# Two-layer graph kernel: ScalarE takes the statistics of the first edge layer's rows, and VectorE's scales go to the end of its turn

## What is computed

```python
def reference(x, src, dst, edge_type_8, L0_gnn_weight, L0_gnn_bias, L1_gnn_W_self, L1_gnn_W_neigh):
    def _L0_gnn_ref(x, edge_index, edge_type, weight, bias):
        row, col = (edge_index[0], edge_index[1])
        xt = jnp.einsum('ni,rio->rno', x, weight)
        messages = xt[edge_type, col]
        out = jax.ops.segment_sum(messages, row, num_segments=num_nodes)
        return jax.nn.relu(out + bias)
    ...
    h = jnp.maximum(_layernorm(x, axis=-1), 0.0)
    x = x + _L0_gnn_ref(h, edge_index, edge_type_8, L0_gnn_weight, L0_gnn_bias)
    h = jnp.maximum(_layernorm(x, axis=-1), 0.0)
    x = x + _L1_gnn_ref(h, L1_gnn_W_self, L1_gnn_W_neigh, src, dst)
    return x
```

## Time and profile before

| | before |
|---|---|
| median of 3 runs | 3427.87 us (3419.07 to 3433.84) |
| profiled execution, its own time | 3424.89 us |
| its span | 3423.2 us |
| granted TensorE clock, mean | 0.912 |
| PE busy | 2528.3 us (74%) |
| DVE busy | 3036.0 us (89%) |
| ACT busy | 2198.9 us (64%) |
| POOL busy | 2461.4 us (72%) |

### The profile page before, as it was taken

The page is one execution under the profiler, slowest core; times in us unless marked ns, Lnnn a source line. Parts: engine busy times, 40 slices in busy tenths (PEclk is TensorE's granted clock), DMA queues, the critical chain, the costliest instruction groups (busy, mean ns, idle before and its releaser), DMA issues.

```text
span 3423.2 us, 64727 instructions
## 1 busy us (share of the span) xinstructions
PE 2528.3 (74%) x10740; PEld 1658.5 (48%) x10741; DVE 3036.0 (89%) x13368; ACT 2198.9 (64%) x6002; POOL 2461.4 (72%) x1732
## 2 busy tenths in 40 slices
PE   3665766767788888888777777777777775777787
PEld 1224655555566666666533333333333333565565
DVE  8999778888899999999789999999999997777777
ACT  5994233323333333333379999999999995777776
POOL 0004886767788888888678888888888885777775
PEclk8998888888899999999989999999999998999989
DMA  9702466666655555555544545445455453889897
GB/s 364 285 0 52 80 116 150 144 139 152 127 105 106 103 106 103 106 103 106 84 155 175 194 173 189 178 173 194 172 186 181 174 190 145 295 285 303 285 306 252
DMA packets 308089, 576.91 MB, mean 169 GB/s; under 512 B 32095, under 2 KB 188034, under 8 KB 307982
## 3 DMA queue, kind: packets, MB, share of 16 engines
q1 hardware_dynamic: 212366, 419.40, 35.9%
q0 software_dynamic: 95616, 156.31, 23.5%
HBM read 316.70 MB, written 258.88 MB: 168 GB/s over the span
## 4 chain that ended last, share of the span: by engine, by line
DVE 45%; issue 24%; PE 15%; DMA 7%; POOL 5%; DVEq 2%; ACT 1%; POOLq 1%; ACTq 0%; SPq 0%
DVE best L1165 6%; DVE w L1172 6%; DVE zone_c L1172 6%; PE banks L1574 5%; DMA agg<-msg,sidx 4%; PE banks L1474 4%; DMA w<-hs,gidx 2%; POOL w L734 2%; PE banks L1416 2%; DVE zone_c L846 2%; DVE zone_c L1050 2%; DVE zone_c L1054 2%; DVE zone_c L848 2%; DVE zone_c L1200 2%; DVE zone_c L1052 2%
## 5 line engine op out<-in xcount | busy, mean ns | idle before, releaser
L1546 PE MATMUL banks<-w,hT 128*128 128x512 f32 x1568 | 764.5, 645 | 252.2 <-ACT hT L1326 247.7
L667 POOL DMA_INDIRECT agg<-msg,sidx x400 | 667.1, 1668 | 185.2 <-issue 123.0
L655 POOL DMA_INDIRECT rows_in<-in_x,gidx x400 | 433.4, 1084 | 414.9 <-DVE gidx L871 280.5
L1546 PEld LDWEIGHTS banks<-w,hT 128*128 128x128 f32 x1568 | 312.8, 204 | 646.0 <-issue 508.7
L1200 DVE SCALAR_TENSOR_TENSOR zone_c<-banks,rdeg,zone_c 128x256 f32 x784 | 379.3, 484 | 158.6 <-PE banks L1574 123.1
L1574 PE MATMUL banks<-w,zone_c 128*128 x1568 | 405.5, 417 | 143.2 <-POOLq L742 113.8
L1416 PE MATMUL banks<-pick,h 128*128 128x128 f32 x1600 | 286.3, 307 | 301.1 <-ACT h L1217 206.1
L1474 PE MATMUL banks<-w,hT 128*128 x1600 | 482.7, 430 | 16.5 <-issue 15.1
L1235 ACT COPY msg<-banks 128x256 f32<-128x256 f32 x400 | 148.2, 370 | 510.9 <-PE banks L1485 486.5
L734 POOL DMA_INDIRECT w<-hs,gidx x392 | 372.5, 950 | 143.5 <-issue 93.8
L1416 PEld LDWEIGHTS banks<-pick,h 128*128 128x128 f32 x1600 | 256.1, 214 | 365.2 <-issue 343.1
(11 more groups left out here) (229 smaller groups left out, 5793.9 us busy)
## 6 DMA issues: line engine op xcount, KB each, us to landing
out_rows<-zone_c SPq DMA_DIRECT2D x196, 512.0 KB, 2.7
agg<-bias SPq DMA_DIRECT2D x2, 25344.0 KB, 97.4
zone_c<-agg SPq DMA_DIRECT2D x98, 512.0 KB, 6.1
hs<-zone_c SPq DMA_DIRECT2D x98, 512.0 KB, 3.6
zone_c<-out_rows SPq DMA_DIRECT2D x98, 512.0 KB, 5.9
rows_in<-in_x SPq DMA_DIRECT2D x97, 512.0 KB, 5.4
keyrow<-key_rows SPq DMA_DIRECT2D x100, 320.0 KB, 3.9
zone_c<-bucket_rows SPq DMA_DIRECT2D x28, 448.0 KB
```

The lines of the kernel that those rows point to most:

```text
L655: pool.indirect_dma_start(out=rows_in[p][:, j, :], out_offset=None, in_=x[:, :], in_offset=bass.IndirectOffsetOnAxis(ap=gidx[p][:, j:j + 1 ...
L667: pool.indirect_dma_start(out=agg[:, :], out_offset=bass.IndirectOffsetOnAxis(ap=sidx[p][:, j:j + 1], axis=0), in_=msg[p][:, j * D:(j + 1) ...
L1546: last = mm(bank[4 + j][:, :], hT[p][:, c, j * P:(j + 1) * P], w1[:, c, :], start=(c == 0), stop=(c == KC - 1))
```

## The change

ScalarE computes the statistics of the first edge layer with three passes over the gathered rows: `edge0_mean` (a copy with a sum, and the sum scaled to minus the mean), `edge0_deviation` (squares with a sum, and std), `edge0_normal` (h, as before). The mean stands behind the third eviction, deviation and normalised tiles behind the fourth. VectorE's bn_stats and bn_aggr go. Its copy of the gather indices, the reciprocal and the shift form `edge0_scales`, which stands at the end of its turn, behind the side work. The mean pass writes its copy into `h`, the square pass into `act_junk`.

```diff
--- before.py
+++ after.py
@@ -269,8 +269,6 @@
         extra = two("extra", [P, B])
         met = two("met", [P, B])
         livekey = two("livekey", [P, B])
-        stats = two("stats", [P, B, 6])
-        mv = two("mv", [P, B, 2])
         std = two("std", [P, B])
         rstd = two("rstd", [P, B])
         shift = two("shift", [P, B])
@@ -392,7 +390,8 @@
         staged0 = sem("staged0")
         node_hot = sem("node_hot")
         degrees0 = sem("degrees0")
-        stats0 = sem("stats0")
+        sum0 = sem("sum0")
+        mean0 = sem("mean0")
         var0 = sem("var0")
         std0 = sem("std0")
         recip0 = sem("recip0")
@@ -894,22 +893,6 @@
             dve.wait_ge(pe_done, 6)
             v.tensor_copy(btype[:, :], bank[3][0:1, 0:SLOTS]).then_inc(btype_done, 1)
 
-            def statistics(b, p, source, stats_sem, var_sem):
-                for j in range(B):
-                    last = v.bn_stats(stats[p][:, j, :], source[p][:, j, :])
-                last.then_inc(stats_sem, 1)
-                wait_alone(dve, stats_sem, b + 1)
-                for j in range(B):
-                    last = v.bn_aggr(mv[p][:, j, :], stats[p][:, j, :])
-                last.then_inc(var_sem, 1)
-
-            def scales(b, p, std_sem, recip_sem, done):
-                dve.wait_ge(std_sem, b + 1)
-                v.reciprocal(rstd[p][:, :], std[p][:, :]).then_inc(recip_sem, 1)
-                dve.wait_ge(recip_sem, b + 1)
-                v.scalar_tensor_tensor(shift[p][:, :], mv[p][:, :, 0], -1.0, rstd[p][:, :], ALU.mult,
-                                       ALU.mult).then_inc(done, 1)
-
 
             def edge0_front(b, r, p):
                 wait_from(dve, sidx0, b - 1, b, 2)
@@ -936,11 +919,15 @@
                                        ALU.mult).then_inc(live0, 1)
                 dve.wait_ge(live0, 2 * b + 1)
                 v.tensor_tensor(livekey[p][:, :], extra[p][:, :], keycol[p][:, :], ALU.add).then_inc(live0, 1)
+
+            def edge0_scales(b, r, p):
+
                 dve.wait_ge(gathered0[p], 16 * B * (r + 1))
                 v.tensor_copy(gidx[p][:, :], from0[:, bass.ds(b * B + 2 * B, B)]).then_inc(staged0, 1)
-                statistics(b, p, rows_in, stats0, var0)
-
-                scales(b, p, std0, recip0, rstd0)
+                dve.wait_ge(std0, b + 1)
+                v.reciprocal(rstd[p][:, :], std[p][:, :]).then_inc(recip0, 1)
+                dve.wait_ge(recip0, b + 1)
+                v.tensor_tensor(shift[p][:, :], minus_mean[p][:, :], rstd[p][:, :], ALU.mult).then_inc(rstd0, 1)
 
             def edge0_cross(b, r, p):
 
@@ -1081,6 +1068,9 @@
                         dve.wait_ge(rank_own, 4 * RCHUNKS)
                         slots_of_positions()
                     sort_hots(c, rc, pc)
+                b, r, p = at.back(0)
+                if inside(b, NBT):
+                    edge0_scales(b, r, p)
 
             phased(dve, PHASES, 2, NBT, edge0_body)
 
@@ -1211,17 +1201,35 @@
         @block.scalar
         def _(act):
 
-            def normalise(b, p, source, rstd_sem, done):
-                act.wait_ge(rstd_sem, b + 1)
+            def edge0_mean(b, r, p):
+
+                act.wait_ge(gathered0[p], 16 * B * (r + 1))
                 for j in range(B):
-                    last = nc.scalar.activation(h[p][:, j, :], source[p][:, j, :], ACT.Relu,
+                    last = nc.scalar.activation(h[p][:, j, :], rows_in[p][:, j, :], ACT.Copy,
+                                                accum_out=total_n[p][:, j:j + 1])
+                last.then_inc(sum0, 1)
+                act.wait_ge(sum0, b + 1)
+                nc.scalar.mul(minus_mean[p][:, :], total_n[p][:, :], -1.0 / D).then_inc(mean0, 1)
+
+            def edge0_deviation(b, p):
+
+                act.wait_ge(mean0, b + 1)
+                for j in range(B):
+                    last = nc.scalar.activation(act_junk[:, j, :], rows_in[p][:, j, :], ACT.Square,
+                                                bias=minus_mean[p][:, j:j + 1],
+                                                accum_out=squares[p][:, j:j + 1])
+                last.then_inc(var0, 1)
+                act.wait_ge(var0, b + 1)
+                nc.scalar.activation(std[p][:, :], squares[p][:, :], ACT.Sqrt, bias=eps[:, 0:1],
+                                     scale=1.0 / D).then_inc(std0, 1)
+
+            def edge0_normal(b, p):
+
+                act.wait_ge(rstd0, b + 1)
+                for j in range(B):
+                    last = nc.scalar.activation(h[p][:, j, :], rows_in[p][:, j, :], ACT.Relu,
                                                 bias=shift[p][:, j:j + 1], scale=rstd[p][:, j:j + 1])
-                last.then_inc(done, 1)
-
-            def edge0_front(b, p):
-                act.wait_ge(var0, b + 1)
-                nc.scalar.activation(std[p][:, :], mv[p][:, :, 1], ACT.Sqrt, bias=eps[:, 0:1]).then_inc(std0, 1)
-                normalise(b, p, rows_in, rstd0, h0)
+                last.then_inc(h0, 1)
 
             def edge0_turned(b, p, q):
                 if q == 0:
@@ -1245,10 +1253,13 @@
                 edge0_evict(b, p, 1)
                 edge0_evict(b, p, 2)
                 if front:
-                    edge0_front(b + 2, p)
+                    edge0_mean(b + 2, r + 1, p)
                 if turn:
                     edge0_turned(b + 1, 1 - p, 1)
                 edge0_evict(b, p, 3)
+                if front:
+                    edge0_deviation(b + 2, p)
+                    edge0_normal(b + 2, p)
 
             def slot_hots(b, r, p):
 
@@ -1267,10 +1278,11 @@
 
             pipeline(act, NB, (slot_hots, 0))
 
-            edge0_front(0, 0)
-            edge0_turned(0, 0, 0)
-            edge0_front(1, 1)
-            edge0_turned(0, 0, 1)
+            for k in range(2):
+                edge0_mean(k, 0, k)
+                edge0_deviation(k, k)
+                edge0_normal(k, k)
+                edge0_turned(0, 0, k)
             pipeline(act, NBT, (edge0_step, 2))
 
 
```

## The result

The changed kernel takes 3710.85 us (median of 4 runs, 3708.85 to 3719.24), the one before 3427.88: a ratio of 1.083 with a 95% interval of 1.0806 to 1.0856, 283 us slower. The profiled execution has a span of 3708.1 us, VectorE 78% busy (89% before), ScalarE 70% (64%), TensorE's mean granted clock 0.871 (0.912).

What follows compares the result with a forecast made beforehand. VectorE's full turn was taken to set the 13.1 us sorting turn, GpSimd close behind; afterwards ScalarE's chain would. Sorting 185 us, ranking 50 and first stretch 25 make 260 on 3427.9: 3688 us, range 3595 to 3775.

Steps and rivals of the forecast that it cites:

- The chain: Edge layer turn: ScalarE's work from the third eviction's start to TensorE's next fold takes 8.44 us, 14.83 us a turn.
- The clock: TensorE, slowed behind a longer gap, brings the third eviction 7.97 us behind the fold, not 6.39: turns of 16.41 us.
- The upper end, 17.4: High end for a turn in us, from the slowest ranking turn behind such a gap, 1.0 us more.
- Ranking: The stretch where slots are ranked: 30 turns, each 1.7 us longer, 50 us.
- first stretch: First 14 turns of the edge layer, including a later first h: 25 us more, ends 10 and 40.
- VectorE's end of turn at nothing: VectorE's scales at its turn's end: ready some 11 us behind a fold, std at about 13.4, so no cost.
- The gathers at nothing: GpSimd's gathers, issued later behind the index copy, still land before ScalarE's mean reads them: no cost.
- The cover of 8 us: Time for the last gather to land: issued near 14 us behind the fold, read at 24.7, 8 us or more.
- GpSimd's 13.0 us as a floor: Sorting stretch: four scatters, four gathers and their issue take 13.0 us; a turn can hardly come below that.
- The signs to look for: Edge layer: VectorE about two thirds busy, waiting some 3 us for std; TensorE gaps 4 to 6 us; sorting clock near 0.84.
- One sign that was to mean: Sorting and ranking stretches: turns of different length would show the forecast wrong; it expected folds 16.4 us apart in both.
- The rival that drew on the most occupied engine: Edge layer: VectorE's relief brings turns to GpSimd's 13.0 us, kernel about 3371 us; chance 0.03.

Runs made afterwards that it cites:

- early order: Changed kernel with ScalarE's mean ahead of the third eviction, deviation and std ahead of the second hT copy and fourth eviction: 3579.84 us beside 3523.77, ratio 1.0161.
- one square of four: Changed kernel with only one of the four square passes, std of all four tiles taken from the first: 3485.09 us beside 3427.53.
- gap filled: Changed kernel with 16 products on constants into an unused bank at the end of each TensorE turn: 3551.16 us beside 3427.53.
- early order and VectorE's part moved back: Changed kernel with mean and deviation one eviction earlier, and VectorE's index copy and scales ahead of its cross masks: 3539.07 us beside 3523.77, ratio 1.0042.
- run by stretch with products: Kernel before, with ScalarE's earlier-placed statistics only from sorting on, VectorE's scales ahead of cross masks, 5 constant products per sorting turn: 3514.95 us beside 3531.97, ratio 0.9956.

## Why the prediction was right

It said 3688 us, 3595 to 3775; the time is 3711. By its own steps:

- **The chain** behind the third eviction: 8.44 us from rows, 8.33 measured in the turn shown (8.32 on the mean of sorting). Its shape is shown three ways: the order alone takes most of the loss back (early order), a shorter pass shortens the turn (one square of four), and with the clock restored a sorting turn is 14.74 us against 14.83 worked out (gap filled).
- **The clock** was the term that was mis-sized. I took the third eviction 7.97 us behind the fold, from a ranking turn with the same gap; it is 8.72, because the slow clock lasts longer behind the fold (0.78 granted over the second 4 us, where that ranking turn has 0.96): the first four fold products take 1.22 us (0.71 in that ranking turn), and the second product is slow too (1.45 us against 1.03). So a turn is 17.05 us, not 16.41, and sorting lost 209 us, not 185. The upper end, 17.4, had covered it.
- **Ranking** 56 us against 50, the **first stretch** with its start 19 against 25.
- **VectorE's end of turn at nothing**: right in the changed kernel (nothing comes back without it), though only because ScalarE's chain covers it. Alone it costs 71 us, and the prediction named the cover but not this price.
- **The gathers at nothing**: right here; ScalarE's mean never waits for them in the list. With the early order and VectorE's part moved back the cover is gone, and the mean waits 1.7 us in most ranking turns. The cover of 8 us was worked out for the longer turns of the changed kernel only: in the kernel before VectorE waited 1.1 us for rows in nearly every ranking turn, which the prediction did not look at.
- **GpSimd's 13.0 us as a floor**: held, 13.01 us in the run by stretch with products. The prediction called GpSimd "close behind" VectorE, whose full turn was to set the 13.1 us; by the same rows GpSimd was full already. That had no part in this result, since ScalarE's chain is longer than both.
- The signs to look for: VectorE at 62% and waiting 3.15 us a turn for std (two thirds and 3), TensorE's gap 3.98 us in sorting and 5.5 in ranking (4 to 6), the load of a table at std once as before, all as said; the clock in sorting 0.80, not 0.84. One sign that was to mean "wrong" did show a little: turns of different length, 17.01 us in sorting and 16.59 in ranking. The third eviction stands nearly alike in both (8.70 and 8.61 us behind the fold on the mean); the 0.35 us in the rest of the turn I can't explain.

The rival that drew on the most occupied engine (faster, 3371 us) fails at its own condition: passes of 4.1 us had to fit in 2.3. What stays open is why a sorting turn settles at 17.05 to 17.1 us almost without spread: I ran nothing that varies the chain in small steps.

## What to carry to other kernels

Before giving work to an idle engine, look at where in that engine's own order its input arrives and its output is wanted. ScalarE was idle two thirds of the time in this layer, but the added passes stood behind the evictions that end a turn and ahead of the tiles that start the next one, and so all of them lay in the loop; the same passes one eviction earlier cost 1.6% instead of 8.3%. The longer gap on TensorE also took its clock here, so price such a gap from a turn that already has one. And when a floor from another engine is on paper, as GpSimd's 13.0 us, don't let a few shorter turns talk you out of it: take the mean over a stretch, and add up that engine's busy time with the short pauses ahead of its instructions. GpSimd's busy share of 80% looked like room and was none.

## What the runs showed of the hardware that was not expected

- TensorE can begin slow behind a gap of only 1.46 us: turns with that same gap take 12.26 us or 13.90 us (granted clock 1.00 or 0.88 over a whole turn), in groups, mostly of three.
- Products without a use, 16 a turn, made the changed kernel 160 us faster; five a turn raised the clock of the kernel before in sorting from 0.94 to 0.98 and made nothing faster.
- GpSimd issues its gathers and scatters 0.3 us apart at the least, so it is full at a busy share of 80%: 604.8 us busy of 752.4, in turns of 13.2 us that need 13.0.
